# Ordering the 128 partitions of a state-space scan group by channel and then state

## The chip, the cores and the metric

One core of one Trainium2 chip runs the whole program. The metric is the device time of one execution in microseconds, and the kernel is run several times. The core has TensorE (PE), VectorE (DVE), ScalarE (ACT) and GpSimd (POOL), the queue of SyncE (SP) that issues every DMA here, and 16 DMA engines that carry them.

## The reference

The reference is a chain of eight layers over x, 8 sequences of 256 tokens with 128 features; after each layer the result is added to x and normalised. The change touches only the first layer, a state-space mixer:

```python
delta = softplus(einsum('blr,dr->bld', dt, dt_proj_w) + dt_proj_b)
A = -exp(A_log)
dA = exp(einsum('bld,dn->lbdn', delta, A))
dBu = einsum('bld,bln,bld->lbdn', delta, Bm, u)
def step(h, t):
    dA_t, dBu_t, c_t = t
    h = dA_t * h + dBu_t
    return (h, einsum('bdn,bn->bd', h, c_t))
```

Here d is one of 128 channels and n one of 16 states: 2048 recurrences per token sequence.

## The kernel before, in words

The tokens are cut into four chunks c of 512 (two sequences each). A chunk goes through stages s = 0 to 7, one for each layer. Three lanes of the on-chip arena hold chunks in flight: chunk 0, chunk 1, and chunks 2 and 3 one after the other. The order of all steps on all engines is worked out when the program is built (`order_of_steps`, line 376 on) from the costs in `PARTS`; each engine then runs its own fixed list and waits on semaphores.

Stage 0 is the mixer. Its 2048 recurrences of a chunk are cut into 16 groups of 128: 8 channels by 16 states, one recurrence for each partition. For each chunk the steps are:

- `0.dt` computes the step size delta and its product with u, both with channels on the partitions. `0.wr` (L848) writes the two as 128 rows of 1024 floats to the DRAM tensor `rep`.
- `0.rp` (L856), once for each group, reads 8 rows of `rep` back into one of `STATES` = 7 ring places of the lane (`ring0`), each row into 16 partitions: 512 KB into 128 partitions of 4 KB. For the first two groups of chunk 2, which is the first to run, this is done on TensorE instead (`0.rb`, with the selection matrix `sel`). So there are 62 loads.
- `0.da` (ACT) takes the exponential of delta times A with per-partition scales `am`, into a PSUM bank.
- `0.db` (POOL, L2118) multiplies the second half of the ring place by B, which `0.bc` has brought to the partition order with the weights `xbc`.
- `0.st` (DVE) runs two scans over 256 tokens (L1728, L1734) and multiplies by C (L1570).
- `0.ac` (PE, L893) sums over the 16 states for four groups at once with the constant `rows8`. When it is done the four ring places may be loaded again: load n of a chunk with n at least 7 waits for `0.ac` number (n - 7) // 4.
- `0.y`, `0.m`, `0.h`, `0.o` and `f` finish the layer, and the later stages follow.

SP issues the loads one after another in the fixed order, after the weight and input loads of the beginning. The loads of chunk 2 come first, then those of chunks 1 and 0 in turn, then those of chunk 3 among the last ones of chunk 0. The next transfer that SP issues after the 62 is the weight load of stage 4 (L826). The other transfers of the program that repeat data are those of the routed layers: L861 writes 7 or 8 rows of 512 to DRAM (`rws`), L868 reads them back as one long row into all 128 partitions, and L873 and L876 fill the rest in stage 7 (source patterns of 48 and of 32 copies).

Of the kernel before, what the change touches and what calls it, by code (L numbers as in the profile page):

```python
# [541 lines left out]
def network(nc, x, ws, cf, cb, rep, rws, out):  # L542
    with ExitStack() as ctx:
# [76 lines left out]
        def ring0(c, q):  # L620
            return ar(c, 3640 + (q % STATES) * 1024, 1024)
# [194 lines left out]
        @block.sync  # L816
        def _(e):
            on = Waits(e)

            def load_x(c):  # L820
                e.dma_start(X[:, c * CH:(c + 1) * CH].rearrange("p (n d) -> p n d", d=128),
                            xv[:, 4 * c:4 * c + 4, :]).then_inc(d_x[c], 16)

            def load_w(s):
                n, at = ws[s].shape[1], W_AT.get(s, 0)
                e.dma_start(W[W_IN[s]][:, at:at + n], ws[s]).then_inc(d_w[s], 16)  # L826

            def stage_over(s):
                for c in range(NC):
                    on.wait_ge(*emptied(u("T", "f", c, s)))  # L830

            load_x(2)
            e.dma_start(CF[:, 0:FIRST], cf[:, 0:FIRST]).then_inc(d_c, 16)
            e.dma_start(W[0][:, 0:FIRST0], ws[0][:, 0:FIRST0]).then_inc(d_w[0], 16)
            load_x(0)
            load_x(1)
            e.dma_start(W[0][:, FIRST0:ws[0].shape[1]], ws[0][:, FIRST0:]).then_inc(d_late, 16)
            e.dma_start(CF[:, FIRST:], cf[:, FIRST:]).then_inc(d_c2, 16)
            load_w(1)
            e.dma_start(CB[:, :].bitcast(mybir.dt.uint16), cb).then_inc(d_cb, 16)  # L840
            load_w(3)
            load_w(2)
            load_x(3)
            for name, s, c, n, _ in order["D"]:
                if name == "0.wr":
                    both = arena[:, LANE[c] * ROOM + S0_AT[3] * 520:LANE[c] * ROOM + S0_AT[3] * 520 + 1040]
                    on.wait_ge(*after("du", "0.dt", c))
                    e.dma_start(rep[c].rearrange("d (k t) -> d k t", k=2),  # L848
                                both.rearrange("p (k x) -> p k x", k=2)[:, :, 0:512]).then_inc(d_wr[c], 16)
                elif name == "0.rp":  # L850
                    g = group0(n)
                    on.wait_ge(d_wr[c], 16)
                    if n >= STATES:
                        y = uses["Y", "0.ac", c, 0]
                        on.wait_ge(full[y.i], y.full - 3 + (n - STATES) // 4)
                    e.dma_start(ring0(c, n), rep[c][8 * g:8 * g + 8, :].unsqueeze(0).to_broadcast([16, 8, 1024])  # L856
                                ).then_inc(repeated(c, n)[0], 16)
                elif name == "ew":
                    E = 7 if s == 1 else 8
                    on.wait_ge(*emptied(u("T", f"{s}.wt", c)))  # L860
                    e.dma_start(rws[ROUTED.index(s) * NC + c][0:E, :], turned(s, c, E)).then_inc(d_ew[c], 16)  # L861
                elif name == "er":
                    E = 7 if s == 1 else 8
                    w, to = rws[ROUTED.index(s) * NC + c], shares_at(s, c)
                    on.wait_ge(d_ew[c], 16 * (ROUTED.index(s) + 1))
                    if s == 1:
                        on.wait_ge(*filled(u("b", "1.rt", c)))
                    e.dma_start(to[:, 0:E * 512], w[0:E, :].rearrange("e t -> (e t)").unsqueeze(0).to_broadcast([128, E * 512])  # L868
                                ).then_inc(d_er[c], 16)
                    if s == 7:  # L870
                        w2 = w.rearrange("(m i) t -> i m t", i=2)
                        for i in range(2):
                            e.dma_start(to[48 * i:48 * i + 48, 4096:6144].rearrange("p (m t) -> p m t", m=4),  # L873
                                        w2[i].unsqueeze(0).to_broadcast([48, 4, 512])).then_inc(d_er[c], 16)
                        ones = cf[0, cmap["one"][0]:cmap["one"][0] + 128]
                        e.dma_start(to[96:128, 4096:6144].rearrange("p (m t) -> p m t", m=16),  # L876
                                    ones.unsqueeze(0).unsqueeze(0).to_broadcast([32, 16, 128])).then_inc(d_er[c], 16)
                else:
                    for q in OVER[s]:
                        stage_over(q)  # L880
                    load_w(s)
            for c in [c for name, _, c, _, p in order["V"] if name == "g" and p]:
                on.wait_ge(*after("zg", "g", c, 7))
                e.dma_start(ov[:, c * 4:(c + 1) * 4, :],
                            rows(8, c).rearrange("p (n d) -> p n d", d=128)).then_inc(d_out, 16)
            e.wait_ge(d_out, 16 * NC)
# [1272 lines left out]
def wide(a, rows=128):  # L2159
    out = np.zeros((128, a.shape[1]), np.float32)  # L2160
    out[0:a.shape[0]] = a
    return out
# [15 lines left out]
def lay_out(i):  # L2178
    g = lambda p: (lambda n: np.asarray(i[p + n]))
    out = []  # L2180
    L = g("L0_attn_")
    xp = L("x_proj_w").T
    out.append({"lng": cols(L("ln1_g")), "lnb": cols(L("ln1_b")), "cxb": cols(L("conv_x_b")),
                "czb": cols(L("conv_z_b")), "dtb": cols(L("dt_proj_b")), "dp": cols(L("Dp")),
                "ln2g": cols(L("ln2_g")), "ln2b": cols(L("ln2_b")), "tap": np.tile(np.concatenate([L("conv_x_w"), L("conv_z_w")], 0)[:, 0, :].T.reshape(1, 1024), (128, 1)),
                "alog": L("A_log").reshape(16, 8, 16).transpose(2, 1, 0).reshape(128, 16), "win": L("in_proj_w").T,
                "xbc": np.repeat(xp[:, 8:40], 8, 1), "sel": np.array([[p % 32 == q % 8 for q in range(128)] for p in range(128)], np.float32), "xdt": wide(xp[:, 0:8].T), "dtw": wide(L("dt_proj_w").T),
                "wout": fold(L("out_proj_w").T, 2), "w1": L("mlp_w1").T, "b1": cols(L("mlp_b1")),
                "w2": fold(L("mlp_w2").T, 4), "b2": row(L("mlp_b2"))})
    L = g("L0_ffn_")  # L2190
# [13 lines left out]
    sel = np.zeros((128,), bool)  # L2204
# [11 lines left out]
    L = g("L1_attn_")  # L2216
    out.append({"wqkv": np.concatenate([L("Wq").T, L("Wk").T, L("Wv").T], 1), "wo": fold(L("Wo").T, 2)})
    L = g("L1_ffn_")
    out.append({"w1": fold(L("w1"), 4), "w2": L("w2"), "b1": cols(L("b1")), "b2": row(L("b2"))})
    L = g("L2_attn_")  # L2220
# [6 lines left out]
    L = g("L2_ffn_")  # L2227
# [29 lines left out]
def constants():  # L2257
    p, q = np.arange(128)[:, None], np.arange(128)[None, :]
    f = lambda a: np.broadcast_to(a, (128, a.shape[-1])).astype(np.float32)
    inv = np.float32(1.0) / np.float32(10000.0) ** (np.arange(0, 4, 2, dtype=np.float32) / np.float32(4))  # L2260
    ang = np.outer(np.arange(256, dtype=np.float32), inv.astype(np.float32)).astype(np.float32)
    cos, sin = np.zeros((128, 256), np.float32), np.zeros((128, 256), np.float32)
    for h in range(16):
        cos[8 * h:8 * h + 4] = 1.0
        for d in range(4):
            cos[8 * h + 4 + d] = np.cos(ang[:, d % 2])
            sin[8 * h + 4 + d] = np.sin(ang[:, d % 2]) * (-1.0 if d < 2 else 1.0)
    sc = np.float32(1.0 / np.sqrt(np.float32(8.0)))
    low = (p < q).astype(np.float32)
    tri = (p <= q).astype(np.float32)  # L2270
    relum = np.concatenate([(q < p) & (q != 0), (q != 0) & (p >= 0), q < p], 1).astype(np.float32)
    outm = np.concatenate([(q > p), np.zeros((128, 128), bool), q > p], 1).astype(np.float32) * np.float32(OUTSIDE)
    outm[outm == 0] = 0.0
    offd = np.concatenate([(q != p), np.ones((128, 128), bool), q != p], 1).astype(np.float32) * np.float32(NEG)
    e, g = np.arange(8)[:, None], np.arange(8)[None, :]
    d = {"ident": f(np.eye(128)), "cosk": cos, "sink": sin, "cosq": cos * sc, "sinq": sin * sc, "low": low,
         "stm": np.concatenate([tri, np.ones((128, 128), np.float32), tri], 1), "relum": relum,
         "outm": outm, "offd": offd, "early": f((g < e).astype(np.float32).reshape(1, 64)),
         "mhalf": f(np.array([[-0.5] * 8 + [0.5] * 8 + [-1.0] * 4])), "one": np.ones((128, 128), np.float32),
         "rows8": np.concatenate([(q[:, 0:32] == 8 * k + p % 8) for k in range(4)], 1).astype(np.float32),  # L2280
         "hm": (p // 8 % 4 == np.arange(4)[None, :]).astype(np.float32)}
    cf = np.concatenate([d[n] for n, _ in CONSTS], 1).astype(np.float32)
    m = np.where(q > p, NEG, 0.0)
    b = {"mask": np.concatenate([m, 0 * m, m], 1)}
    cb = np.concatenate([b[n] for n, _ in CONSTB], 1).astype(np.float32)
    cb = (np.ascontiguousarray(cb).view(np.uint32) >> 16).astype(np.uint16)
    return cf, cb
# [21 lines left out]
```

## Time and profile before

| | us |
|---|---|
| median of 3 runs | 1457.04 |
| lowest and highest run | 1456.47, 1458.47 |
| the profiled execution, its own time | 1458.54 |
| its span in the profile | 1456.7 |
| TensorE busy in it | 1296.2 |
| VectorE busy in it | 1043.7 |

The profile is of one execution. Its own time holds 1.8 us ahead of and behind the span. All times quoted from the trace count from the start of the span. Busy shares are means over stages of very different kinds. The mixer takes about the first 225 us for the four chunks; the stages behind it are what fills the rest.

### The profile page before, as it was taken

The page shows a single profiled execution, that of the slowest core. Times are in us where ns is not written, and L with a number is a line of the kernel's source. Part 1 is how long each engine was busy: PE and PEld are TensorE (multiplying, and loading weights), DVE is VectorE, ACT ScalarE, POOL GpSimd, SP SyncE. Part 2 cuts the span into 40 slices and gives each one's busy share as a digit, 9 for nine tenths or more (in the row PEclk, how much of TensorE's full clock was granted, in tenths as well). Part 3 has the DMA queues.
Part 4 walks back from the last instruction along what each step waited for, and adds up shares of the span by engine and source line. Part 5 has one row for each costly group of instructions (what it writes and reads, how often), then busy time and mean ns, then how long its engine had stood idle before and what let it go on. Part 6 is the DMA issues. An engine that isn't in the chain of part 4 may idle for free.

```text
span 1456.7 us, 26022 instructions
## 1 busy us (share of the span) xinstructions
PE 1296.2 (89%) x8638; PEld 913.3 (63%) x8638; DVE 1043.7 (72%) x3814; ACT 894.7 (61%) x2479; POOL 693.2 (48%) x699
## 2 busy tenths in 40 slices
PE   8445647988998999999999999999999999999998
PEld 4122324666565666767767677687777787866565
DVE  5878796789676875687688775378988688666324
ACT  6553747689768746465877776436657648654211
POOL 1355443457456744355454655555516315433354
PEclk9756778799999999999999999999999999999999
DMA  7797660100201011000000102201010000030800
GB/s 260 181 225 179 174 144 1 65 2 2 102 1 52 2 52 60 1 1 1 1 1 2 60 1 86 92 1 59 9 69 1 2 1 1 1 88 16 253 1 22
DMA packets 21789, 82.88 MB, mean 57 GB/s; under 512 B 1852, under 2 KB 8252, under 8 KB 19352
## 3 DMA queue, kind: packets, MB, share of 16 engines
q1 hardware_dynamic: 21656, 81.23, 19.2%
q8 instruction: 69, 1.13, 0.3%
q14 instruction: 64, 0.52, 0.1%
HBM read 77.88 MB, written 3.33 MB: 56 GB/s over the span
## 4 chain that ended last, share of the span: by engine, by line
PE 55%; DVE 25%; ACT 6%; POOL 6%; issue 4%; DMA 3%; SPq 1%; DVEq 0%; POOLq 0%; ACTq 0%
PE bank L893 48%; PE bank L897 7%; DVE arena L1570 7%; ACT arena L1330 4%; DVE arena L1807 3%; DVE arena L1805 2%; DMA arena<-rep 2%; POOL arena L2155 2%; DVE arena L2066 1%; DVE arena L1728 1%; DMA arena<-cf 1%; DVE arena L1573 1%; DVE arena L1734 1%; DVE arena L2059 1%; DVE stats L1584 1%
## 5 line engine op out<-in xcount | busy, mean ns | idle before, releaser
L1330 ACT ACTIVATE arena<-arena 128x256 f32<-128x256 f32 (+2 forms) x792 | 347.8, 443 | 77.4 <-DVE arena L1807 45.0
L1330 ACT ACTIVATE arena<-bank 128x512 f32<-128x512 f32 (+4 forms) x351 | 189.4, 569 | 250.5 <-PE bank L893 152.4
L893 PE MATMUL bank<-XT,W 128*128 128x512 f32 (+1 forms) x752 | 295.5, 529 | 2.4 <-DVE arena L1570 1.0
L2154 POOL TENSOR_TENSOR arena<-arena 128x256 f32<-128x256 f32 x192 | 119.9, 625 | 336.2 <-DVE arena L1822 335.6
L893 PEld LDWEIGHTS bank<-W,arena 128*128 128x128 f32 x1888 | 234.5, 195 | 59.5 <-issue 46.9
L893 PE MATMUL bank<-W,arena 128*128 128x128 f32 (+1 forms) x1888 | 245.3, 280 | 11.3 <-POOL arena L2127 4.4
L893 PE MATMUL bank<-arena 128*32 128x256 f32 (+8 forms) x2912 | 239.0, 335 | 13.6 <-DVE arena L1828 4.4
L2127 POOL TENSOR_TENSOR arena<-arena 128x512 f32<-128x512 f32 (+1 forms) x108 | 170.9, 1602 | 111.1 <-DVE arena L1570 40.1
L893 PEld LDWEIGHTS bank<-arena 128*32 128x32 f32 (+4 forms) x2912 | 157.8, 151 | 91.8 <-issue 59.5
L897 PE MATMUL bank<-CF,arena 128*128 128x128 f32 x1312 | 185.0, 282 | 33.8 <-ACT arena L1330 16.2
L897 PEld LDWEIGHTS bank<-CF,arena 128*128 128x128 f32 x1312 | 151.4, 145 | 85.4 <-issue 72.4
L2155 POOL TENSOR_TENSOR arena<-arena 128x512 f32<-128x512 f32 x192 | 203.7, 1061 | 0.0
L893 PEld LDWEIGHTS bank<-XT,W 128*128 128x128 f32 x752 | 134.5, 192 | 88.6 <-issue 79.0
L1330 ACT ACTIVATE arena<-bank,W 128x512 f32<-128x512 f32 (+1 forms) x192 | 109.5, 617 | 75.8 <-PE bank L893 58.9
L893 PE MATMUL bank<-arena,W 128*128 128x512 f32 (+3 forms) x288 | 144.7, 650 | 10.2 <-ACT arena L1330 6.3
L1330 ACT ACTIVATION_READ_ACCUMULATOR arena<-arena 128x1 f32 x768 | 145.3, 189 | 0.0
L1570 DVE TENSOR_TENSOR arena<-bank,arena 128x512 f32<-128x512 f32 x98 | 65.4, 686 | 94.0 <-PE bank L893 81.1
L1828 DVE COPY arena<-bank 128x512 f32<-128x512 f32 x157 | 103.1, 683 | 38.4 <-PE bank L897 37.5
L2118 POOL TENSOR_TENSOR arena<-arena 128x512 f32<-128x512 f32 x62 | 78.8, 1278 | 93.6 <-DMA arena<-rep 93.6
L1330 ACT ACT_TABLE_LOAD x79 | 101.4, 1283 | 32.8 <-DVE arena L1570 9.8
L1570 DVE TENSOR_TENSOR arena<-arena 128x4 f32<-128x4 f32 (+5 forms) x244 | 103.0, 427 | 13.5 <-DVE arena L1807 0.5
L1807 DVE CUSTOM_DVE_ANT_0 arena<-bank,CB 128x256 f32<-128x256 f32 x256 | 107.3, 419 | 0.0
(124 smaller groups left out, 1652.7 us busy)
## 6 DMA issues: line engine op xcount, KB each, us to landing
arena<-rep SPq DMA_DIRECT2D x62, 512.0 KB, 8.4
arena<-rws SPq DMA_DIRECT2D x8, 2048.0 KB, 7.7
arena<-rws SPq DMA_DIRECT2D x4, 1792.0 KB, 6.5
W<-w SPq DMA_DIRECT2D x2, 2124.0 KB, 8.4
arena<-rws SPq DMA_DIRECT2D x8, 384.0 KB, 13.1
W<-w SPq DMA_DIRECT2D x1, 2692.0 KB, 9.2
W<-w SPq DMA_DIRECT2D x1, 2256.5 KB, 8.7
rep<-arena SPq DMA_DIRECT2D x4, 512.0 KB, 3.5
```

The lines of the kernel that those rows point to most:

```text
L893: return e.matmul(o, lhsT, rhs, start=start, stop=stop, skip_group_check=True)
L897: ins = e.transpose(bank[b.i][:, j * 128:j * 128 + s.shape[0]], s, cst("ident"))
L1330: return e.activation(o, a, func, **kw)
L1570: return e.tensor_tensor(o, a, b, op)
L1573: return e.tensor_scalar(o, a, s1_, s2_, op0, op1) if op1 is not None else e.tensor_scalar(o, a, s1_, None, op0)
L1805: e.tensor_tensor_reduce(px[:, j * 384:j * 384 + 128], bank[b.i][:, 0:128], bias[:, 0:128], -1.0, 3.4e38, ALU.add, ALU.min, nm[:, 2 * j:2 ...
L1807: e.tensor_tensor_reduce(px[:, j * 384 + 128:(j + 1) * 384], bank[b.i][:, 128:384], bias[:, 128:384], -1.0, 3.4e38, ALU.add, ALU.min, nm[: ...
L1828: e.tensor_copy(third(s, c, n), bank[b.i][:, :]).then_inc(done[b.i], 1)
L2118: e.tensor_tensor(h, h, s0(c, 8), ALU.mult).then_inc(has["dB"], 1)
L2127: e.tensor_tensor(h, h, w, ALU.mult).then_inc(has["gw"], 1)
L2154: e.tensor_tensor(px[:, :, 0:128], px[:, :, 0:128], rec[:, :, 0:1].to_broadcast([128, 2, 128]), ALU.mult)
L2155: e.tensor_tensor(px[:, :, 128:384], px[:, :, 128:384], rec[:, :, 1:2].to_broadcast([128, 2, 256]), ALU.mult).then_inc(has["pn"], 1)
```

## The change

Partition p of a group held state p // 8 of channel p % 8 of the group. After the change it holds channel p // 16 and state p % 16. The load of a group, which repeated the block of 8 rows 16 times over, now repeats each row 16 times before the next. The host-made arrays `alog` (the A of each partition), `xbc` (weights that give B and C on each partition), `sel` and the constant `rows8` are laid out to match. Their sizes, and all other instructions and the order of the steps, are as they were.

```diff
@@ -853,7 +853,7 @@
-                    e.dma_start(ring0(c, n), rep[c][8 * g:8 * g + 8, :].unsqueeze(0).to_broadcast([16, 8, 1024])
+                    e.dma_start(ring0(c, n), rep[c][8 * g:8 * g + 8, :].unsqueeze(1).to_broadcast([8, 16, 1024])
                                 ).then_inc(repeated(c, n)[0], 16)
@@ -2183,8 +2183,8 @@
-                "alog": L("A_log").reshape(16, 8, 16).transpose(2, 1, 0).reshape(128, 16), "win": L("in_proj_w").T,
-                "xbc": np.repeat(xp[:, 8:40], 8, 1), "sel": np.array([[p % 32 == q % 8 for q in range(128)] for p in range(128)], np.float32), "xdt": wide(xp[:, 0:8].T), "dtw": wide(L("dt_proj_w").T),
+                "alog": L("A_log").reshape(16, 8, 16).transpose(1, 2, 0).reshape(128, 16), "win": L("in_proj_w").T,
+                "xbc": np.concatenate([np.tile(xp[:, k:k + 16], 8) for k in (8, 24)], 1), "sel": np.array([[p % 32 == q // 16 for q in range(128)] for p in range(128)], np.float32), "xdt": wide(xp[:, 0:8].T), "dtw": wide(L("dt_proj_w").T),
@@ -2277,7 +2277,7 @@
-         "rows8": np.concatenate([(q[:, 0:32] == 8 * k + p % 8) for k in range(4)], 1).astype(np.float32),
+         "rows8": np.concatenate([(q[:, 0:32] == 8 * k + p // 16) for k in range(4)], 1).astype(np.float32),
```

## Rows read from the trace of the kernel before

**Rows 1.** The page: span, busy engines, and bytes moved in 40 slices.

```profile
span 1456.7 us, 26022 instructions
...
PE 1296.2 (89%) x8638; PEld 913.3 (63%) x8638; DVE 1043.7 (72%) x3814; ACT 894.7 (61%) x2479; POOL 693.2 (48%) x699
...
GB/s 260 181 225 179 174 144 1 65 2 2 102 1 52 2 52 60 1 1 1 1 1 2 60 1 86 92 1 59 9 69 1 2 1 1 1 88 16 253 1 22
```

**Rows 2.** Busy time by windows; the last columns are TensorE clock, DMA share, GB/s.

```profile
core 0: us, PE busy (x) PEld busy (x) DVE busy (x) ACT busy (x) POOL busy (x), PEclk, DMA share, GB/s
10.00:19.00 9.00, 8.32 (x21) 4.08 (x22) 4.18 (x24) 5.11 (x9) 2.09 (x2) 0.81 1.00 424
64.00:84.00 20.00, 3.87 (x16) 0.48 (x17) 14.56 (x24) 5.47 (x7) 8.85 (x7) 0.50 0.93 221
84.00:116.00 32.00, 20.44 (x76) 12.36 (x76) 23.59 (x46) 19.94 (x26) 18.75 (x16) 0.60 1.03 233
116.00:136.00 20.00, 4.08 (x20) 1.13 (x20) 19.21 (x42) 5.77 (x10) 13.17 (x12) 0.60 0.87 204
815.00:819.00 4.00, 3.05 (x8) 1.21 (x8) 2.14 (x3) 3.99 (x7) 4.00 (x4) 1.00 0.95 393
```

**Rows 3.** Timeline of POOL: first of a run of seven multiplications, and the last.

```profile
98.57 1.26 POOL L2118 TENSOR_TENSOR arena<-arena 128x512 f32<-128x512 f32 x1 [0.24 <-DMA arena<-rep]
...
111.89 1.27 POOL L2118 TENSOR_TENSOR arena<-arena 128x512 f32<-128x512 f32 x1 [0.99 <-DMA arena<-rep]
```

**Rows 4.** Waits from 26 to 217 us: engine, line, releaser; total, times, longest.

```profile
POOL arena L2118 <- DMA arena<-rep: 93.6, 43, 21.3
...
SPq L856 <- PE bank L893: 113.6, 11, 18.0
```

**Rows 5.** The chain that ended last, from 44 to 86 us: start, us, what.

```profile
48.20 8.56 DMA arena<-rep
...
56.82 1.28 POOL arena L2118
...
58.13 0.69 DVE arena L1728
58.82 0.59 DVE arena L1734
...
59.51 0.70 DVE arena L1570
...
60.34 1.97 PE bank L893 x8
...
62.33 4.89 DMA arena<-rep
...
74.61 9.76 DMA arena<-rep
```

**Rows 6.** DMA issues: count, KB each, median us from issue to landing.

```profile
arena<-rep SPq DMA_DIRECT2D x62, 512.0 KB, 8.4
...
rep<-arena SPq DMA_DIRECT2D x4, 512.0 KB, 3.5
...
rws<-arena SPq DMA_DIRECT2D x8, 16.0 KB
...
rws<-arena SPq DMA_DIRECT2D x4, 14.0 KB
```

**Rows 7.** Timeline of POOL at the first load's landing and at the last one's.

```profile
34.54 1.27 POOL L2118 TENSOR_TENSOR arena<-arena 128x512 f32<-128x512 f32 x1 [21.30 <-DMA arena<-rep]
...
216.16 1.26 POOL L2118 TENSOR_TENSOR arena<-arena 128x512 f32<-128x512 f32 x1 [4.64 <-DMA arena<-rep]
```

**Rows 8.** Timeline of DVE: the last group's two scans and its product with C.

```profile
220.30 0.69 DVE L1728 TENSOR_TENSOR_SCAN arena<-bank,arena 128x256 f32<-128x256 f32 x1
220.91 0.66 DVE L1734 TENSOR_TENSOR_SCAN arena<-bank,arena 128x256 f32<-128x256 f32 x1
221.68 0.69 DVE L1570 TENSOR_TENSOR arena<-arena,bank 128x512 f32<-128x512 f32 x1
```

## The prediction

> **What bounds the kernel now.** I read the page first, then the windows of the first 225 us, the waits of POOL and SP there, and the chain. The page shows a kernel whose TensorE is busy 1296.2 of 1456.7 us, but the bytes moved stand in the first six slices, 174 to 260 GB/s, and nearly nowhere else [rows 1]: the first six slices of 36 us are the mixer, and there TensorE is busy 3.87 of 20 us and 4.08 of 20 [rows 2]. That stage has a limit of its own, and it is where the change lies.
>
> The windows show it. From 84 to 116 us the DMA engines are busy all the time (share 1.03) and move 233 GB/s; from 64 to 84 it is 0.93 and 221 [rows 2]. These are the loads of `rep`. From 10 to 19 us the engines carry weights with a share of 1.00 and move 424 GB/s, and at 815 us one row repeated into all 128 partitions comes at 393 with 0.95 [rows 2]. So full engines move little more than half as much in the mixer's loads, and repetition of a source is not the reason. In time: from the first to the last of seven multiplications of POOL, each of which waits for its load, 13.32 us pass, so one load of 512 KB takes 2.22 us [rows 3]. POOL waits 93.6 us for these loads [rows 4]. For chunk 2 three such waits, 8.56, 4.89 and 9.76 us, stand on the chain [rows 5]. Later VectorE is as close: busy 19.21 of 20 us from 116 on [rows 2]. So the mixer is held by the loads first, and then by VectorE with the loads just behind it.
>
> **The change, part by part.** The arrays `alog`, `xbc`, `sel` and `rows8` keep their sizes, and every matmul, activation, multiplication and scan keeps shape and place. Which recurrence sits in which partition changes no instruction's length, since all 128 partitions are worked at once. I count zero for them, above and below; nothing has to hide them. No step is moved and no issue is added: SP still issues 62 loads.
>
> What is left is the source pattern of the 62 loads. It was 16 copies of a block of 8 rows; it becomes 8 rows of 16 copies each. The outermost count falls from 16 to 8. I expect the load then to run on 8 of the 16 engines. What bears on it in the trace: the page gives a time to landing for each kind of transfer except the two kinds of `rws<-arena`, and these are the ones whose outermost count is 8 or 7 [rows 6]. I read that as a completion that sixteen engines' signals don't make up. It is an inference, and its failure is a rival below.
>
> [...]
>
> Now the price. Each of 8 engines has to carry 64 KB of a load (65.5 thousand bytes) where each of 16 carried 32. No row shows such a load, so I bound it. If an engine keeps the pace that it has in these loads, a load takes twice 2.22 = 4.44 us. If it runs at the pace of the weight loads, 424 / 16 = 26.5 GB/s for each engine, it takes 2.47 us. Both bounds are above the present 2.22; with 16 engines at that pace it would be 1.24. I take 4.44. Whatever halves the pace of these loads is not the source, for the repeated row at 393 GB/s has the same source for all partitions; what is left as special, by my reading of the pattern, is that each engine gets a block of neighbouring partitions (8 of them, one copy of the 8 rows). With 8 engines a block is 16 neighbouring partitions: the same thing, wider.
>
> [...]
>
> **The sum.** All times are in the profiled execution. Today the queue has gaps: SP waits 113.6 us for `0.ac` to free ring places [rows 4]. At 4.44 us these close. From the landing of a load to the next issue that it allows there are 1.28 on POOL, 1.28 of scans, 0.70 for the product and 1.97 of PE, with joints 5.6 us (56.76 to 62.33) [rows 5]. The four groups that free the places leave three later loads of the seven-place ring in flight, 13.3 us of work, so the queue doesn't run dry. Hence from the first load on it is one train:
> - The first load landed just before 34.54 [rows 7]; it will take 2.22 longer: 36.8.
> - 61 more at 4.44: 270.8, to 307.6.
> - Three writes of 512 KB to `rep` (chunks 0, 1 and 3) run in the same train, at the 424 GB/s 1.24 each: 3.7, to 311.3.
> - Today the last lands just before 216.16 [rows 7]. The difference is 95.1 us.
> - Behind the last landing stand 6.2 us up to the end of the product with C (221.68 + 0.69) [rows 8], since VectorE is crowded. With the train as the limit it is not, and the path is 1.26 + 0.69 + 0.66 + 0.69 = 3.3 [rows 7, 8]: 2.9 back. It leaves 92.2.
>
> Is any of it hidden? Each engine keeps its fixed list. Work of stage 1 for chunk 1 is spread among the mixer's steps and goes ahead or waits with them; the bulk of TensorE's 1296 us stands behind the last `0.ac`, so it starts later by the whole amount. What waits behind a late load is, on POOL, the small steps of the layer norms of other chunks, on ACT `0.da` and the evictions behind it, on VectorE the scans, and from them `0.ac` on TensorE. All this is in the train already. The later weight loads have hundreds of us of room. TensorE's granted clock is 0.50 to 0.60 where it waits much [rows 2]; more waiting leaves it there longer, and I add 1 us. Sum: 93 us. The profiled execution's own time of 1458.54 is 1.5 above the median of 1457.04; on the median the forecast is **1550 us**.
>
> **The rivals.**
> - *Eight engines at full pace.* With half the engines whatever slows them against each other may vanish; 2.47 us a load. For: the weight loads' pace. Against: the pace is low in every mixer window. Price: 0.25 us more a load. In the 52 us from 64 to 116, where the queue is full, are 23 loads, 6 us, and chunk 2's first 13 add 3; VectorE hides the rest later. About 1466. [...] This case decides from the point where eight engines no longer slow each other; a partly eased slowing, 3 to 4 us a load, lies between 1475 and 1525.
> - *Nothing changes.* The load is still dealt to 16 engines in blocks of eight partitions: 2.22 us a load, 1457. Against: the outermost count, and the missing landings.
> - *Faster.* Sixteen engines stay and the new order lets them run without slowing each other: 1.24 us a load. Place: the three DMA waits on the chain, 23.2 us together [rows 5]; at 1.24 for 2.22 they lose 10. VectorE, busy 19.21 of 20 us from 116 on, takes back half: 1452. It decides when more than about half of the loads speed up. Against it speaks what speaks against the rival above.
>
> **How the numbers follow.** Forecast 0.66 (its own range 1525 to 1580: 4.0 us a load takes 27 off; 4.95, twice the 2.47, adds 31), eight engines with little or no slowing 0.16, unchanged 0.10, faster 0.08. To leave no more than 2 in 10 out, the range has to reach the second case: 1460 to 1580. A measurement can tell 0.2%, 2.9 us, from no change. Slower by more: 0.66 + 0.14 = 0.80. Within: 0.10 + 0.02 = 0.12. Faster: 0.08.
>
> **What would show it.** In the profile after: the DMA share in the mixer's busy windows near 0.5, at about 118 GB/s; POOL's multiplications 4.4 us apart while they wait; no time to landing for `arena<-rep`; the last of them at about 311 us; VectorE's and TensorE's totals as now. If the share is near 1, the engines stayed sixteen; if it is 0.5 at 200 GB/s and more, the second case holds. The prediction is wrong if the spacing is near 2.5 us, or if the stages behind the mixer take up part of the 93 us.

## The result, and the profile after

The changed kernel takes 1503.18 us (median of 4 runs, 1484.4 to 1508.97) against 1457.13 for the kernel before; the ratio that goes with it, 1.023 (1.015 to 1.031), counts only the two faster of the four runs, 1484.4 and 1497.88. A second measurement, below, in which all six runs count, gave 1.031 (1.028 to 1.034). So it is slower by some 46 us where 93 had been forecast, and its runs spread over 24 us where those of the kernel before spread over 2.

The profiled execution took 1508.49 us. Its page, the lines that answer to [rows 1] and to the chain:

```profile
span 1506.7 us, 26022 instructions
...
PE 1297.7 (86%) x8638; PEld 912.7 (61%) x8638; DVE 1047.0 (69%) x3814; ACT 895.9 (59%) x2479; POOL 695.3 (46%) x699
...
GB/s 241 162 133 129 165 141 149 8 63 1 2 99 2 50 1 50 58 1 1 2 1 1 35 24 1 171 1 57 2 74 2 1 1 1 2 85 0 250 10 22
...
PE 51%; DVE 20%; DMA 12%; ACT 6%; POOL 5%; issue 3%; SPq 1%; DVEq 0%; POOLq 0%; ACTq 0%
```

No engine has more work: TensorE is at 1297.7 us for 1296.2. The mixer's bytes fill seven slices where they filled six, at a lower rate, and DMAs hold 12% of the chain. The windows that answer to [rows 2], and one more:

```profile
64.00:84.00 20.00, 1.97 (x11) 0.23 (x8) 11.67 (x19) 4.69 (x6) 7.59 (x6) 0.50 0.50 162
84.00:116.00 32.00, 8.41 (x36) 4.47 (x36) 17.88 (x35) 7.77 (x13) 10.75 (x10) 0.55 0.51 126
116.00:136.00 20.00, 12.32 (x48) 7.33 (x48) 9.80 (x15) 11.89 (x15) 7.18 (x7) 0.78 0.51 128
171.00:193.00 22.00, 14.17 (x38) 4.86 (x36) 17.42 (x26) 18.40 (x22) 10.75 (x9) 0.81 0.47 188
```

The DMA share was 1.03 and is 0.51, that of half the engines at work. But look at the last column. With about the same share the loads move 126 GB/s in one stretch and 188 in another. POOL's multiplications, the answer to [rows 3] and [rows 7], show it load by load:

```profile
86.06 1.26 POOL L2118 TENSOR_TENSOR arena<-arena 128x512 f32<-128x512 f32 x1 [3.27 <-DMA arena<-rep]
90.27 1.27 POOL L2118 TENSOR_TENSOR arena<-arena 128x512 f32<-128x512 f32 x1 [2.94 <-DMA arena<-rep]
94.45 1.27 POOL L2118 TENSOR_TENSOR arena<-arena 128x512 f32<-128x512 f32 x1 [2.92 <-DMA arena<-rep]
...
179.79 1.27 POOL L2118 TENSOR_TENSOR arena<-arena 128x512 f32<-128x512 f32 x1 [1.20 <-DMA arena<-rep]
182.31 1.27 POOL L2118 TENSOR_TENSOR arena<-arena 128x512 f32<-128x512 f32 x1 [1.25 <-DMA arena<-rep]
184.76 1.26 POOL L2118 TENSOR_TENSOR arena<-arena 128x512 f32<-128x512 f32 x1 [1.18 <-DMA arena<-rep]
...
267.04 1.26 POOL L2118 TENSOR_TENSOR arena<-arena 128x512 f32<-128x512 f32 x1 [3.83 <-DMA arena<-rep]
```

4.2 us a load at 90 us, 2.5 us at 180. Over the whole train nearly all loads are of these two kinds, 3.8 to 4.2 us or about 2.5, with a few between where the pace changes: near the two bounds of the prediction's price, and the kernel runs at both in turn. The last load lands at 267.0 where it landed at 216.2, 50.9 us later, and the span grew by 50.0.

After the first nine loads SP issues the others in two long trains: 34 from 64.08 us on and, behind the write of chunk 3 to `rep`, the last 19 from 192.90 us on. The waits of POOL and SP from 26 to 270 us, as in [rows 4], and the DMA issues, as in [rows 6]:

```profile
POOL arena L2118 <- DMA arena<-rep: 162.7, 62, 22.7
SPq L856 <- PE bank L893: 109.6, 11, 16.4
```

```profile
arena<-rep SPq DMA_DIRECT2D x62, 512.0 KB
```

All 62 loads are now waited for, 162.7 us for 93.6, and the page no longer gives them a time to landing. SP waits for `0.ac` as long as before, 109.6 us for 113.6.

### The profile page after: what moved, and what is told of

It is laid out like the page before. It is cut to its first block, busy times and chain, and to the rows that moved or that the text cites. A ratio compares the mean times of both kernels' runs of the same rounds, so it can differ in the third digit from the quotient of the medians.

```text
span 1506.7 us, 26022 instructions
## 1 busy us (share of the span) xinstructions
PE 1297.7 (86%) x8638; PEld 912.7 (61%) x8638; DVE 1047.0 (69%) x3814; ACT 895.9 (59%) x2479; POOL 695.3 (46%) x699
## 4 chain that ended last, share of the span: by engine, by line
PE 51%; DVE 20%; DMA 12%; ACT 6%; POOL 5%; issue 3%; SPq 1%; DVEq 0%; POOLq 0%; ACTq 0%
PE bank L893 44%; DMA arena<-rep 10%; PE bank L897 7%; DVE arena L1570 6%; ACT arena L1330 4%; DVE arena L1807 3%; DVE arena L1805 2%; POOL arena L2155 2%; ACT L1330 1%; DVE arena L2066 1%; DMA arena<-cf 1%; DVE arena L2059 1%; SPq L856 1%; DVE arena L1828 1%; DVE stats L1584 1%
## 5 line engine op out<-in xcount | busy, mean ns | idle before, releaser
L2118 POOL TENSOR_TENSOR arena<-arena 128x512 f32<-128x512 f32 x62 | 80.1, 1292 | 162.7 <-DMA arena<-rep 162.7
L1330 ACT ACTIVATE arena<-bank,W 128x512 f32<-128x512 f32 (+1 forms) x192 | 109.0, 617 | 55.8 <-PE bank L893 50.9
L1330 ACT ACTIVATE bank<-arena,am 128x512 f32<-128x512 f32 x62 | 48.3, 782 | 127.3 <-DMA arena<-rep 126.6
L1330 ACT ACT_TABLE_LOAD x79 | 101.4, 1283 | 32.3 <-DVE arena L1570 9.8
```

Of the source, the lines that this page charges most:

```text
L1330: return e.activation(o, a, func, **kw)
L2118: e.tensor_tensor(h, h, s0(c, 8), ALU.mult).then_inc(has["dB"], 1)
```

## Experiments

Each was timed beside the kernel before on the same chip, whose medians there were 1455.4 to 1456.8 us (one run of it, of 4486.53 us, stays unexplained). A time given without a range is that of a single run. The three kernels with 128 different rows compute something else and serve for their times alone.

**Sixteen engines with the new order.** Each row goes to DRAM twice, so that a load has 16 outer rows again.

```diff
-e.dma_start(rep[c].rearrange("d (k t) -> d k t", k=2),
-            both.rearrange("p (k x) -> p k x", k=2)[:, :, 0:512]).then_inc(d_wr[c], 16)
+for r in range(2):
+    e.dma_start(rep[c].rearrange("(d r) (k t) -> r d k t", r=2, k=2)[r],
+                both.rearrange("p (k x) -> p k x", k=2)[:, :, 0:512]).then_inc(d_wr[c], 16)
...
-rep[c][8 * g:8 * g + 8, :].unsqueeze(1).to_broadcast([8, 16, 1024])
+rep[c][16 * g:16 * g + 16, :].unsqueeze(1).to_broadcast([16, 8, 1024])
```

> The partition order of the change (channel, then state) is kept. Each row is written to DRAM twice, so that the load has sixteen rows of eight copies as its pattern: the outermost count is 16 again, and each channel's row is still read for neighbouring partitions one after the other. Theory: the cost of the change is the number of engines alone. Then the loads come 2.2 us apart while POOL waits for them, the DMA share is near 1.0 at about 235 GB/s between 84 and 116 us, landings are printed again, and the time is 1457 to 1462 (the second write is 1.24 us for each chunk). Rival: the order in which rows are read (one row many times in a row) costs the time, whatever the number of engines. Then the time stays at 1485 to 1509.

Measured: 1458.57 us (10 runs, 1456.85 to 1463.02), ratio 1.002 (1.000 to 1.003). The window, and the landings, which are back:

```profile
84.00:116.00 32.00, 20.95 (x76) 12.64 (x76) 23.35 (x46) 19.94 (x26) 18.69 (x16) 0.58 1.01 238
```

```profile
arena<-rep SPq DMA_DIRECT2D x62, 512.0 KB, 7.8
```

The partition order is that of the change, and the cost is gone. What costs is the outermost count of 8 in the source pattern and what hangs on it: half the engines and, by the prediction's reading of the pattern, wider blocks of neighbouring partitions. How much is due to which, this kernel doesn't tell; the kernels with narrower blocks below do. The order of the reads costs nothing that can be measured. 8 outermost gave a share of 0.51, 16 gave 1.01.

**What lowers the pace of an engine.** Two kernels that load 128 different rows in place of 8 repeated ones, once with 128 rows outermost, once with the same rows as 16 by 8. Both are the kernel before but for this line, one of the two new ones in each (the recurrences so get rows of other channels):

```diff
-rep[c][8 * g:8 * g + 8, :].unsqueeze(0).to_broadcast([16, 8, 1024])
+rep[c]                                          # 128 in front
+rep[c].rearrange("(a b) t -> b a t", b=16)      # 16 in front
```

> The kernel before, with each load reading all 128 rows of the chunk, one for each partition, in place of 8 rows sixteen times; the recurrences so get the rows of other channels, a changed computation of equal size. The outermost count is 128. Theory: the pace of 2.22 us a load comes from how the partitions are dealt to the engines when the outermost count is 16, and 128 is dealt as in the weight loads. Then a load takes about 1.24 us: the loads move 380 to 424 GB/s while the share is near 1. The time is 1445 to 1456. Rival: 4 KB packets into these places are slow as such. Then 235 GB/s and 2.22 us stay.

> As the run with 128 in front, 128 different rows for each load (the same changed computation up to the order of rows), but taken as sixteen outer by eight inner rows. Theory: the dealing into blocks of eight neighbouring partitions makes the pace, not the repetition of the source. Then 2.2 us a load and about 235 GB/s at a share near 1, time about 1457. Rival: the sixteen reads of the same 8 rows contend at the source. Then about 1.24 us a load, as with 128 in front.

Measured: 1456.93 and 1455.97 us. The windows from 84 to 116 us, first with 128 in front:

```profile
84.00:116.00 32.00, 18.41 (x76) 12.05 (x76) 24.92 (x48) 19.58 (x26) 16.91 (x15) 0.72 0.63 239
```

then with 16 in front:

```profile
84.00:116.00 32.00, 20.61 (x76) 12.49 (x76) 23.52 (x46) 19.94 (x26) 18.72 (x16) 0.59 1.03 237
```

The same bytes need a share of 0.63 in one and 1.03 in the other. While busy, the engines move 239 / 0.63 = 379 GB/s with 128 outer rows and 230 with 16, though every row is read once in both. So it is what goes with the outermost count, by the prediction's reading how the partitions are dealt to the engines, and not a repeated source, that lowers the pace, in the kernel before too. The two kernels also differ in the order in which the rows are read, but with 16 in front the pace is the same for rows in three different orders: 233 GB/s in the kernel before, 238 with the doubled rows, 237 here. No trace names the engine of a packet, so that 16 in front means blocks of neighbouring partitions stays the prediction's reading. And a second thing: loads that are much faster left the time where it was, 1456.93 us where 1445 to 1456 had been expected, in the one run there is.

**Eight engines with narrow blocks.** Each load as four DMAs of 32 partitions, by the same reading a block of 4 for each engine. This expectation and several below suppose pairs of engines that slow each other while they are in step. That is a conjecture of the author; no run shows such pairs.

```diff
-e.dma_start(ring0(c, n), rep[c][8 * g:8 * g + 8, :].unsqueeze(1).to_broadcast([8, 16, 1024])
+for q4_ in range(4):
+    e.dma_start(ring0(c, n)[32 * q4_:32 * q4_ + 32, :],
+                rep[c][8 * g:8 * g + 8, :].unsqueeze(1).to_broadcast([8, 4, 1024])
```

> Each load is issued as four DMAs of 32 partitions with eight outer rows of four copies: partition p holds channel p % 32 // 4, and the host arrays are laid out to match. [...] 62 loads become 248 issues of about 0.6 us on SP, 2.4 us a load. Theory (in-step pairs): loads come 2.5 us apart, all the time, share near 0.5 at about 205 GB/s, time 1460 to 1475, and little spread from run to run. Rival (eight engines have a slow and a fast pace for another reason): 4.0 us a load in part of the mixer, 1480 to 1510 and a spread as the change shows.

Measured: 1463.95 us (1461.15 to 1465.4), ratio 1.004 (1.002 to 1.006).

```profile
84.00:116.00 32.00, 17.35 (x70) 10.23 (x67) 23.31 (x44) 18.80 (x25) 16.61 (x15) 0.63 0.50 188
```

188 GB/s at a share of 0.50, 2.8 us a load and not the 2.5 expected, with 248 issues on SP. No slow stretch: from 64 to 200 us it is 183 GB/s at 0.49. Eight engines at nearly full pace (376 GB/s for one unit of share, 424 for the weight loads) cost 7 us, not 46: of the price of the change the smaller part is the number of engines, and the rest is the low pace that they keep for long stretches in the changed kernel.

**Does the place of the partitions matter?** Two kernels with three DMAs for each load, equal in count, size and block: the wide one of 64 partitions begins at 32 in one and at 0 in the other. What the two expectations call the port theory is the conjecture on pairs in step; the author expected the one from 0 to be the slower by it.

```diff
+for p0, m in ((0, 4), (32, 8), (96, 4)):        # from 32
+for p0, m in ((0, 8), (64, 4), (96, 4)):        # from 0
+    e.dma_start(ring0(c, n)[p0:p0 + 8 * m, :],
+                rep[c][8 * g:8 * g + 8, :].unsqueeze(1).to_broadcast([8, m, 1024])
```

> Each load is three DMAs on eight engines: partitions 0 to 31 (blocks of 4), 32 to 95 (blocks of 8) and 96 to 127 (blocks of 4), each with eight rows outermost; the host arrays are laid out to match, and the whole computation is kept. SP issues 186 DMAs, about 1.8 us a load, less than the 2.47 us that the engines need. [...] Port theory: loads come 2.5 to 2.7 us apart all the time, above 195 GB/s from 84 to 116 us, time 1457 to 1466 with a spread below 8 us. Rival (blocks of eight neighbours or more are slow on eight engines, wherever they lie): the middle DMA is slow, 3.3 to 3.6 us a load, about 150 GB/s, 1470 to 1490.

> The same three DMAs but for the place: partitions 0 to 63 (blocks of 8), 64 to 95 and 96 to 127 (blocks of 4). Sizes, engines and issues are as in the run that starts its wide DMA at 32. [...] Port theory: 8 of the 16 packets of each engine go in pairs, so about 8 x 0.28 + 8 x 0.155 = 3.5 us a load while in step, near 150 GB/s in the stretches in step; time 1465 to 1490. Rival (only counts and block sizes matter): the same pace as the run that starts at 32.

Measured: 1462.27 us (1461.2 to 1463.66) and 1463.53 (1459.82 to 1464.86). The two times can't be told apart. The windows at the starts of the two long trains of loads can. From 32:

```profile
64.00:84.00 20.00, 1.93 (x8) 0.23 (x8) 12.49 (x20) 4.69 (x6) 7.22 (x6) 0.50 0.48 176
84.00:116.00 32.00, 17.49 (x58) 8.29 (x59) 22.58 (x43) 18.63 (x24) 16.68 (x15) 0.61 0.52 198
...
166.00:186.00 20.00, 12.43 (x60) 7.13 (x60) 15.00 (x32) 13.31 (x19) 11.58 (x11) 0.74 0.51 201
```

From 0:

```profile
64.00:84.00 20.00, 2.94 (x16) 0.23 (x8) 12.37 (x20) 3.62 (x6) 6.02 (x6) 0.50 0.45 142
84.00:116.00 32.00, 14.35 (x49) 6.93 (x52) 22.72 (x44) 17.21 (x24) 17.23 (x15) 0.66 0.51 197
...
166.00:186.00 20.00, 12.52 (x39) 6.24 (x38) 15.34 (x33) 9.78 (x15) 8.72 (x8) 0.63 0.52 171
```

For one unit of share: 176 / 0.48 = 367 and 394 GB/s from 32, 316 and 329 from 0, and 386 from 0 once the train has run for a while. With the wide DMA from 0 the loads are slower in both starts than with it from 32. That is the order that was expected, but no trace shows engines that slow each other from 0 and not from 32. It is one trace of each kernel, too, and the wide DMA also stands first in one load and second in the other. The slowing ends sooner than in the changed kernel (208 GB/s from 97 to 116 us), so it costs next to nothing here. The first kernel came as its theory had it; for the second 1463.53 lies just below the forecast of 1465 to 1490, and the pace of 150 GB/s that was behind it was not met (142 and 171 at the starts, 197 between), a miss.

**The source again, on eight engines.** The changed kernel with 128 different rows as 8 by 16.

> The changed kernel with each load reading 128 different rows, as eight outer by sixteen inner rows; a changed computation of equal size. Eight engines, sixteen neighbouring partitions each. Theory: the source plays no part, so 4.0 to 4.2 us a load while in step (126 GB/s), with or without a fast stretch. Rival (reading one row sixteen times in a row is what slows an engine): 2.5 us a load, about 205 GB/s at a share of 0.5, all the time.

Measured: 1493.67 us, with both paces:

```profile
84.00:116.00 32.00, 8.71 (x36) 4.66 (x36) 18.24 (x35) 7.09 (x12) 10.08 (x10) 0.50 0.51 125
174.00:190.00 16.00, 10.72 (x35) 3.43 (x33) 12.88 (x20) 15.08 (x19) 8.29 (x6) 0.93 0.51 206
```

Reading one row sixteen times in a row is not what slows an engine either.

**Pushing the pairs out of step.** Before four of chunk 2's loads two extra DMAs; `k` is 2 and 6 in the one kernel, 4 and 4 in its control. The 2 and 6 were meant to put one engine of each pair a block of four packets behind the other, the 4 and 4 to delay both alike. That rests on the conjecture and on a guess of the author at the engines that take the rows of a small DMA; no trace names them.

```diff
+if (c, n) in ((2, 2), (2, 7), (2, 11), (2, 15)):
+    for k in (2, 6):
+        e.dma_start(scr[len(shifts)][0:k, :], ws[4][0:k, 0:4096]).then_inc(d_st, 16)
```

> The changed kernel with two small extra DMAs ahead of four of chunk 2's loads (2, 7, 11 and 15): a copy of 2 rows of 16 KB from DRAM to DRAM, and one of 6 rows. [...] Theory (the pairs slow each other only while in step): the loads behind them come 2.5 us apart from 73 us on, the DMA share is near 0.5 at over 190 GB/s between 84 and 116 us, where the changed kernel had 126, and the time is 1458 to 1485, depending on whether the queue runs empty later. Rival (eight engines change between two paces for reasons that have nothing to do with step): 126 to 135 GB/s in that window as in the changed kernel, 1484 to 1509.

> The control of the run before: at the same four places two extra DMAs of 4 rows each, the same 8 rows of 16 KB in all. [...] Theory: the pace stays as in the changed kernel, 4.0 to 4.2 us a load and about 126 GB/s from 84 to 116 us. Rival (any disturbance lets the engines go): above 190 GB/s there, as in the run before.

Measured: 1475.87 us (1468.35 to 1477.96), ratio 1.015 (1.013 to 1.016), and one run of the control at 1472.46. With 2 and 6:

```profile
64.00:84.00 20.00, 1.94 (x8) 0.23 (x8) 7.90 (x13) 3.13 (x4) 5.35 (x5) 0.50 0.50 134
84.00:116.00 32.00, 13.84 (x44) 6.67 (x44) 24.01 (x46) 16.96 (x23) 17.55 (x15) 0.65 0.51 209
```

With 4 and 4:

```profile
64.00:84.00 20.00, 1.93 (x8) 0.23 (x8) 11.23 (x18) 3.13 (x4) 5.53 (x5) 0.50 0.38 133
84.00:116.00 32.00, 14.06 (x44) 6.75 (x44) 20.32 (x40) 13.98 (x19) 16.28 (x14) 0.60 0.51 189
```

The first long train ran at 209 GB/s, as the theory had it. But the third of the four pushes left the loads at 134 GB/s with a share of 0.50, and the control, whose expectation was 126, ran at 189. Its third push even let the engines go at once: 133 GB/s at a share of 0.38 are 350 for one unit of share. So the simple form of the theory, that a push must set the partners of a pair apart by a block, is contradicted. From 84 to 116 us the loads are fast in both traces with extra DMAs and slow, 125 to 134 GB/s, in the four without (the changed kernel's three and the one with 8 by 16 different rows), so a disturbance ahead of the train seems to let the engines go. More than that can't be said. The last train has no push just ahead of it and turned fast early too (205 GB/s from 190 to 210 us with 2 and 6). And the gain in time is not shown: on this chip two of the changed kernel's own runs took 1467.41 and 1489.65 us (below), and 1475.87 and 1472.46 lie between them.

**The same push with sixteen engines.** The kernel before with `k` 4 and 12, meant as the offset between the engines of a pair was above.

> [...] Theory: the loads may run at up to 1.24 us (over 300 GB/s at a share near 1) in the window from 84 to 116 us while the offset lasts. Rival (sixteen engines fall back into step, as no trace of them showed a fast stretch): 235 GB/s there. Either way the time stays within 4 us of the kernel before, since 128 rows in front gave the fast loads and no gain.

Measured: 1459.32 us.

```profile
84.00:116.00 32.00, 17.32 (x59) 8.84 (x60) 24.16 (x47) 19.59 (x26) 20.35 (x18) 0.61 1.00 235
```

Sixteen engines stay at 235 GB/s. None of their traces has a fast stretch with 16 in front (233, 238 and 237 GB/s in the others).

**The changed kernel twice more.**

> The changed kernel as it is, for its spread and a second trace. Theory: two paces, about 4.0 us and 2.5 us a load, and switches between them at other moments than in the first trace; the time goes with the share of loads at the slower pace, anywhere from 1470 to 1515. Rival (the switch belongs to a place in the program, such as a write to DRAM or a stage): the fast stretches lie where they lay, at 73 to 82, 170 to 193 and 252 to 262 us.

> The changed kernel once more, for its ratio and its spread. Theory (two paces, the switch at chance moments): runs anywhere from 1465 to 1510, median near 1490; the trace has stretches of about 126 to 136 GB/s and of about 210 GB/s at the same share of 0.5, and the last load lands between 225 and 270 us according to how long the slow ones last. Rival (the first measurements' spread came from the chips used): a spread below 8 us on this chip.

In the first of the two the profiled execution took 1749.88 us, with TensorE's granted clock at 0.75 from 600 us on, and its trace is used for the loads alone; the other runs were 1467.41, 1489.65 and 2642.52, the last unexplained. In the trace the loads were still at 134 GB/s from 84 to 116 us and at 195 from 116 to 136. The second gave 1503.28 us (6 runs, 1490.82 to 1507.29), ratio 1.031 (1.028 to 1.034). Its runs spread over 16 us on the one chip, so the spread doesn't come of different chips. Its windows:

```profile
84.00:116.00 32.00, 8.54 (x36) 4.60 (x36) 18.27 (x35) 7.79 (x13) 10.76 (x10) 0.55 0.51 129
136.00:156.00 20.00, 7.11 (x26) 2.69 (x27) 18.99 (x48) 9.44 (x15) 12.93 (x12) 0.56 0.51 210
180.00:230.00 50.00, 16.73 (x72) 8.18 (x72) 32.13 (x75) 18.69 (x28) 21.53 (x19) 0.63 0.52 132
```

and its last load:

```profile
250.51 1.26 POOL L2118 TENSOR_TENSOR arena<-arena 128x512 f32<-128x512 f32 x1 [3.02 <-DMA arena<-rep]
```

Here the loads were fast from about 120 us to the end of the first long train, where the first trace was slow until 170: in this train the switch does not belong to a place in the program. In the last train it may. All three traces of the changed kernel are slow there up to its last few loads and have three at about 2.5 us ahead of the very last, from 254, 238 and 242 us on. That is what the rival of the first of the two expectations says, so it is refuted for the first long train alone. The last load came 34.4 us later than in the kernel before, and this execution took 1490.82 us, 32.3 more than that of before (1458.54); in the first trace it was 50.9 and 50.0. So in both the time follows the last load, and the spread of the runs is by all appearance that of the moment of the switch.

The traces show one thing that goes with the switch. Now and then a packet of 8 KB comes on a queue that the profile calls `q14 instruction`. In the first trace one starts at 166.0 us, here in the window from 165 to 168:

```profile
q14 instruction: 1, 0.01, 1.2%
```

The multiplications of POOL around it start 4.24, 3.32, 2.91 and 2.61 us apart (from 164.24 us on). Take the long trains of six traces: the changed kernel's three, the 8 by 16 different rows, and the two with extra DMAs, these for the last train alone. The loads go over to the fast pace eleven times, and ten times the first interval below 3.7 us ends 2 to 8 us after the start of such a packet; between 60 and 262 us a trace has only six or seven of them. The exception is the short fast stretch at 74 us of the first trace, which follows the write to `rep`. The kernel with the wide DMA from 0 moved 178 GB/s from 86 to 95 us and 208 from 97 to 116, with a packet at 95.6. On the other hand many such packets change little: those at 111.4 and 213.6 us of the first trace left the loads slow (4.07 and 3.83 us a load behind them), and those in the kernel before, as at 94.5 us, do nothing (2.3 us a load up to 89.00 us, 2.2 from 98.57 us on). No run adds or leaves out such a packet, so that it sets off the switch is not shown.

## Why the prediction was right and where it was wrong

The half of it that held: nothing but the 62 loads changed; they run on eight engines (share 0.51, no landings, and the cost gone with sixteen rows outermost); they become nearly one train that the mixer waits for, with two holes of about 1 us at 80 and 192 us; the stages behind take up none of the delay. Landing to end of span is 1239.7 us now (1506.7 - 267.0) and was 1240.5. The two small terms at the end, 2.9 us back behind the last landing and 1 us for the clock, came to 0.9 back in place of 1.9. One reading on the way was not sound: the prediction took SP's wait of 113.6 us for `0.ac` as the gaps of the queue and had them close. The gaps did close, and SP still waits 109.6 us, for it waits while several loads are in flight.

The rows of no cost are borne out by the kernel with doubled rows: `alog`, `xbc`, `sel` and `rows8` in the new order cost nothing beside what can be measured.

What failed is one term of the sum, "61 more at 4.44". With the three writes the prediction gave the train 274.5 us, and it took 230.6 (from 36.44, the first multiplication, to 267.04). It was mis-sized in two ways.
- At the low pace the loads were a little quicker than twice 2.22: 46 came 4.06 us apart in the mean, not 4.44, the writes of chunks 0 and 1 included. That is 17 us.
- It held one pace for the whole train. 14 loads of the first trace came at 2.60 in the mean (3 from 73.66 us, 8 from 171.80 and 3 from 254.31), 1.84 less than the forecast each, 26 us. The two are the 43 of the 44 us by which the last landing, forecast at 311.3, came early at 267.0.

The prediction had both bounds, 2.47 and 4.44, and asked which of the two holds. It was the wrong question: the kernel has both paces and stays at either for tens of microseconds. A value between, 3 to 4 us a load, was named as a partly eased slowing and priced at 1475 to 1525, but got no chance of its own; the mean over the 61 loads is 3.8 and the time 1503.18. So the price was right for the mean, while the mechanism, two paces in turn, was in none of the cases. Why the low pace is 4.06 us and not 4.44, the runs don't say. No row of the kernel before shows two paces.

The second case, eight engines at full pace for about 1466 us, was worked out well: the two kernels that come near that pace all the time take 1462.27 and 1463.95, with more DMAs to issue. It also shows where the 46 us lie: some 7 in the number of engines, and the rest, nearly 40, in the low pace. The faster case was worth less than its 5 us: loads at 379 GB/s left the time at 1456.9. The chain showed 23.2 us of DMA waits [rows 5], but what was gained there was given back before the mixer ended; VectorE, busy 19.21 of 20 us behind it [rows 2], and 19.20 in that kernel, is the likely taker, though it is one run, and no run took VectorE's work away.

What stays open is what moves the engines from the lower pace to the higher one. Seen is: a train tends to begin slow, after the queue has been empty (in the first trace the share is 0.01 from 192 to 193 us, and the loads behind it come 4.02 us apart); it then goes fast at a moment that differs from run to run (in the first long train of the changed kernel's three traces the first interval below 3.7 us ends at 171.80, 122.01 and 118.91 us); in the long trains no trace shows it falling back before the engines have stood idle; ten of eleven times it comes within 8 us behind a packet of `q14 instruction`; with extra DMAs ahead the first long train was fast in two traces of two, whichever engines they were meant for; and sixteen engines with 16 in front were never seen to go (233 to 238 GB/s). That the lower pace comes of pairs of engines in step stays the author's conjecture: the starts with the wide DMA from 0 were slower than those from 32 (316 and 329 GB/s for one unit of share, 367 and 394), and blocks of four had no slow stretch, but neither the pairs nor the step was measured. The sum for the wide DMA from 0 has 8 of the 16 packets of an engine go in pairs at 0.28 us each; no run shows that term, and in its place the loads of the first start came 3.24 us apart (from 70.83 to 90.27 us) where the sum gave 3.5.

## What to carry to other kernels

Look at the outermost count of the pattern when the copies of a repeated source are reordered: a change of layout that made it 8 in place of 16 halved the DMA share here (1.03 to 0.51), and set the engines to a low pace besides (126 GB/s from 84 to 116 us); 16 outer rows in the new order brought back 1.01 and 238 GB/s. With 16 in front the loads still ran at 0.6 of the pace of a pattern with 128 in front (230 for 379 GB/s), so read GB/s beside the DMA share, never the share alone. And when a term lies between two bounds with a mechanism for each, allow for a kernel that visits both, and for a time that spreads.

## What was not expected of the hardware

One and the same program loads at 126 or at 210 GB/s (15.8 or 26.3 for each engine) with eight busy engines, mostly for 20 to 80 us at a time, with the same instructions all along; runs of the one kernel lie between 1467.41 and 1508.97 us, 2.8% apart, where fourteen runs of the kernel before on one chip lie within 0.7%. The pace goes up within 8 us behind a packet of the queue `q14 instruction`, ten times of eleven; no run puts that to the test. And sixteen engines in this dealing (235 GB/s) are hardly quicker than eight at their faster pace (210).
